# Two depthwise convolutions with group norm: border rows read straight into the taps, small values in PSUM, and a third crossed channel moved from ScalarE and GpSimd to VectorE

## The chip, the cores and the metric

One core of one Trainium2 chip. The metric is device time in microseconds of the core; before the change it was measured three times, with a median of 431.45 us.

## The reference

The input x is 4 x 96 x 128 x 128 in fp32. Twice, the kernel adds to x a convolution of its group norm:

```python
x = x + _L0_conv_ref(_gn(x), w1, w3, w5, alpha)   # alpha0*x + alpha1*dw1(x) + alpha2*dw3(x) + alpha3*dw5(x)
x = x + _L1_conv_ref(_gn(x), w, b)                # one 3x3 filter and one bias for all channels
```

`_gn` takes 32 groups of three channels, each with mean and variance over the three channels and the whole picture. The first convolution is depthwise, and its four terms fold into one 5x5 filter per channel. The second is a 3x3 filter shared by all channels. The kernel calls them X and Y.

## The kernel before

**Tiling.** A unit is two groups, one on partitions 0 to 63 (LO), one on 64 to 127 (HI); each partition holds two picture rows, row p and row p + 64, as two halves of the free dimension, for 4 images and 3 channels of 128 columns. There are 16 units (NU) and 18 periods: in period i the kernel convolves X of unit i and Y of unit i - 2 (LAG). xt holds four pairs of units; x is loaded, updated in place by both convolutions, and stored from it.

**TensorE.** A convolution along the rows is a banded 64 x 64 matrix for each horizontal tap. The normalised input is split into a high and a low fp16 part, gn_hi and gn_lo, and the filter of the high part into two, so a channel takes 15 band products for X and 9 for Y. `tiles` (L382) issues each product as four 64x64 matmuls, two halves of the picture for both groups; for half 1 the output goes to the other group's partitions (LO input to HI output). Those outputs are called crossed. The rows beyond a 64-row strip come through halo, a tile in which each border row stands once for each tap and part, and one more product (`edge`). Group sums over partitions are products with constant matrices (`mean_product`, L443; `var_product`) into the PSUM tile ps_s; it waits for norm_step (L446) before it overwrites ps_s.

**VectorE.** Per period and in this order: `evacuate` of Y's channel 1 of unit i - 3, `deviations` (L652 to L664), Y's channel 2, `affine` (L666 to L688), statistics of x for unit i + 2 (L649), nine evictions for X (three channels, each an uncrossed half on 128 partitions and two crossed quarters on 64), statistics of Y, and Y's channel 0. An eviction (L703) multiplies a PSUM bank by a scale, adds xt and writes xt. In `deviations` the mean is reduced from ps_s, subtracted from the partial means and the difference squared; `affine` turns the variance into g_mul and g_add with a reciprocal and a Newton step. In the last period before the end VectorE also does `whole_part` (L718) and `low_split` (L727) for the last unit, between `affine` and the part (1, 2) of Y's channel 2.

**ScalarE.** `root` (L538), the square root of each unit; `normalize`, 16 activations per period (gn_f in fp32, gn_hi in fp16); `cross_over` (L569), which copies a crossed half of Y from PSUM to the tile cross on the right partitions. With NCROSS = 3 all three channels of Y go this way, and VectorE evicts only their uncrossed halves. The crossing of channel 2 stands right behind `root` of the next period.

**GpSimd.** `low_part` (L870), gn_lo = gn_f - gn_hi, eight per period; `cross_add` (L879), which adds cross to xt.

**SyncE's queue** issues nearly all DMAs in a hand-written order and waits for semaphores in line: `edges_out` (L206, L212, L216) writes the border rows of gn to edge_scratch in DRAM; `edges_spread` (L228) copies them within DRAM to tap_scratch, once per tap and shifted by one column each; `edges_in` (L240, L242) loads tap_scratch to halo, four DMAs; `load_band` (L307) loads the band matrices, `save_pair` (L288) writes filters, `load_pair` (L254) and `store_pair` (L267) move x in and out in alternate periods, batch by batch. In period j the order is: edges_in X of j; edges_out Y of j - 2; bands; filters in even periods; edges_spread Y; load or store of batch 0; edges_in Y; batch 1; edges_out X of j + 1; batch 2; edges_spread X of j + 1; batch 3. A store waits until both the evictions and the cross additions of its unit are done (`unit_ready`). The first four units are loaded one by one, unit 2 by ScalarE's queue (L248); the last unit's border rows go through ScalarE's queue, and so do two of its stores.

## Time and profile before

| | us |
|---|---|
| three runs: lowest, median, highest | 429.09, 431.45, 433.03 |
| the profiled execution | 433.64 |
| its span | 431.8 |
| VectorE busy | 336.6 (78%) |
| TensorE busy | 317.9 (74%) |
| ScalarE busy | 305.3 (71%) |
| GpSimd busy | 261.9 (61%) |

The span runs from the first to the last instruction of the profiled execution. A busy share is an average over start, middle and end, so it doesn't name the limit of any of them; the waits and the timelines do. L-numbers are lines of the kernel before. PE is TensorE, DVE VectorE, ACT ScalarE, POOL GpSimd, SP SyncE; a q behind a name is the queue in which an engine issues DMAs. A bracket at the end of a timeline row is the engine's idle time before it and what ended it.

### The profile page before, as it was taken

The page shows a single profiled execution, that of the slowest core. Times are in us where ns is not written, and L with a number is a line of the kernel's source. Part 1 is how long each engine was busy: PE and PEld are TensorE (multiplying, and loading weights), DVE is VectorE, ACT ScalarE, POOL GpSimd, SP SyncE. Part 2 cuts the span into 40 slices and gives each one's busy share as a digit, 9 for nine tenths or more (in the row PEclk, how much of TensorE's full clock was granted, in tenths as well). Part 3 has the DMA queues.
Part 4 walks back from the last instruction along what each step waited for, and adds up shares of the span by engine and source line. Part 5 has one row for each costly group of instructions (what it writes and reads, how often), then busy time and mean ns, then how long its engine had stood idle before and what let it go on. Part 6 is the DMA issues. An engine that isn't in the chain of part 4 may idle for free.

```text
span 431.8 us, 12518 instructions
## 1 busy us (share of the span) xinstructions
PE 317.9 (74%) x5184; PEld 260.3 (60%) x5184; DVE 336.6 (78%) x667; ACT 305.3 (71%) x374; POOL 261.9 (61%) x207
## 2 busy tenths in 40 slices
PE   2285967819887986988878879688797888983910
PEld 2163645709776865677756767577576788862600
DVE  7868998828979895999699898979898959698110
ACT  1407651499989788779896979697887979835330
POOL 6405632287878676758784867666776868644311
PEclk9997788969999899799989999999899999998865
DMA  7697497104976798678868795779667247404855
GB/s 151 176 241 203 121 230 188 25 31 126 229 188 181 212 218 214 171 216 208 211 174 228 186 241 154 187 209 238 186 178 226 63 142 188 142 18 107 220 144 146
DMA packets 115517, 74.66 MB, mean 173 GB/s; under 512 B 5564, under 2 KB 110916, under 8 KB 115460
## 3 DMA queue, kind: packets, MB, share of 16 engines
q1 hardware_dynamic: 108720, 70.49, 64.2%
q10 hardware_dynamic: 6740, 3.37, 3.4%
q8 instruction: 41, 0.67, 0.7%
q14 instruction: 16, 0.13, 0.1%
HBM read 46.35 MB, written 32.74 MB: 183 GB/s over the span
## 4 chain that ended last, share of the span: by engine, by line
DMA 37%; SPq 29%; DVE 12%; ACT 10%; issue 4%; PE 3%; POOL 2%; ACTq 1%; POOLq 0%
DMA tap_scratch<-edge_scratch 19%; DMA edge_scratch<-gnX 10%; SPq L242 6%; SPq L212 5%; DVE xt L703 5%; SPq L307 5%; ACT gn_f L559 4%; SPq L240 4%; DVE stats L649 4%; ACT gnX L560 3%; DMA xt<-in_x_dram 3%; PE ps L387 3%; SPq L267 2%; SPq L216 2%; SPq L254 2%
## 5 line engine op out<-in xcount | busy, mean ns | idle before, releaser
L387 PE MATMUL ps<-gnX,band 64*64 64x512 f16 x2880 | 187.2, 407 | 28.9 <-DVE xt L703 14.5
L387 PEld LDWEIGHTS ps<-gnX,band 64*64 64x64 f16 x2880 | 157.9, 189 | 53.1 <-issue 39.3
L703 DVE SCALAR_TENSOR_TENSOR xt<-ps,unscale,xt 128x512 f32<-128x512 f32 (+1 forms) x192 | 142.3, 747 | 34.9 <-PE ps L387 32.5
L649 DVE BATCH_NORM_STATS2 stats<-xt 128x6 f32<-128x384 f32 x256 | 121.0, 545 | 17.3 <-DMA xt<-in_x_dram 16.7
L559 ACT ACTIVATE gn_f<-xt,g_add,g_mul 128x768 f32<-128x768 f32 x120 | 122.1, 1017 | 12.6 <-DVE g_add L687 12.0
L870 POOL TENSOR_TENSOR gnX<-gn_f,gnX 128x768 f16<-128x768 f32 x60 | 92.6, 1544 | 60.6 <-ACT gnX L560 60.6
L870 POOL TENSOR_TENSOR gnY<-gn_f,gnY 128x768 f16<-128x768 f32 x60 | 92.6, 1544 | 32.5 <-ACT gnY L560 32.5
L387 PE MATMUL ps<-gnY,band 64*64 64x512 f16 x1728 | 105.3, 386 | 2.1 <-DVE xt L703 2.0
L387 PEld LDWEIGHTS ps<-gnY,band 64*64 64x64 f16 x1728 | 87.0, 187 | 15.7 <-issue 3.9
L879 POOL TENSOR_TENSOR xt<-xt,cross 128x512 f32<-128x512 f32 x48 | 61.3, 1279 | 57.7 <-ACT cross L569 57.3
L569 ACT ACTIVATE cross<-ps,unscale 64x512 f32<-64x512 f32 x96 | 65.5, 682 | 36.7 <-PE ps L387 35.1
L560 ACT ACTIVATE gnX<-xt,g_add,g_mul 128x768 f16<-128x768 f32 x64 | 64.7, 1015 | 1.1 <-DVE g_add L687 1.1
L560 ACT ACTIVATE gnY<-xt,g_add,g_mul 128x768 f16<-128x768 f32 x64 | 64.7, 1015 | 0.0
L538 ACT ACTIVATE std<-var,eps_t 128x8 f32<-128x8 f32 x19 | 5.7, 301 | 61.2 <-DVE var L670 61.0
L387 PE MATMUL ps<-haloX,halo_wX 60*64 60x512 f16 x192 | 18.5, 420 | 19.8 <-DMA haloX<-tap_scratch 19.7
L387 PE MATMUL ps<-haloY,halo_wY 35*64 35x512 f16 x192 | 17.2, 404 | 20.4 <-DMA haloY<-tap_scratch 20.4
L387 PEld LDWEIGHTS ps<-haloY,halo_wY 35*64 35x64 f16 x192 | 6.1, 111 | 26.3 <-DMA haloY<-tap_scratch 23.7
L387 PEld LDWEIGHTS ps<-haloX,halo_wX 60*64 60x64 f16 x192 | 5.4, 110 | 25.5 <-DMA haloX<-tap_scratch 24.8
L449 PE MATMUL ps_s<-stats,ones_mean 64*64 64x32 f32 x76 | 5.8, 224 | 15.7 <-DVE stats L649 15.7
L449 PEld LDWEIGHTS ps_s<-stats,ones_mean 64*64 64x64 f32 x76 | 5.9, 142 | 17.8 <-DVE stats L649 8.8
L456 PE MATMUL ps_s<-stats,ones_var 64*64 64x96 f32 x76 | 7.6, 275 | 11.0 <-DVE stats L663 10.9
L456 PEld LDWEIGHTS ps_s<-stats,ones_var 64*64 64x64 f32 x76 | 5.1, 143 | 16.1 <-DVE stats L663 15.7
(75 smaller groups left out, 107.8 us busy)
## 6 DMA issues: line engine op xcount, KB each, us to landing
out_dram<-xt SPq DMA_DIRECT2D x56, 384.0 KB, 4.7
xt<-in_x_dram SPq DMA_DIRECT2D x48, 384.0 KB, 5.8
band<-diag_scratch SPq DMA_DIRECT2D x48, 160.0 KB, 2.8
tap_scratch<-edge_scratch SPq DMA_DIRECT2D x16, 246.9 KB, 4.1
haloX<-tap_scratch SPq DMA_DIRECT2D x32, 123.4 KB
xt<-in_x_dram SPq DMA_DIRECT2D x20, 192.0 KB, 4.2
xt<-in_x_dram ACTq DMA_DIRECT2D x12, 192.0 KB, 6.6
out_dram<-xt SPq DMA_DIRECT2D x12, 192.0 KB, 3.6
```

The source lines that it names most:

```text
L212: eng.dma_start(edge_dram[s][p, g, :, side, :, :].rearrange("h r e -> r h e"), src).then_inc(edges_landed[s], 16)
L240: eng.dma_start(halo[s][R * g:R * g + 2 * n, p, :, :, :].rearrange("r b c w -> r (b c w)")[:, 0:EDGE], tap_dram[s][p, g, :, :, 0:EDGE].rea ...
L242: eng.dma_start(halo[s][R * g + 2 * n:R * g + 3 * n, p, :, :, :].rearrange("r b c w -> r (b c w)")[:, 0:EDGE], tap_dram[s][p, g, 0, :, 0:E ...
L307: sp.dma_start(band5[:, i % 2, c, :], bass.AP(win.tensor, win.offset + (R // WIN - 1) * NM, [[RUN, 2 * WIN], [-NM, R // WIN], [1, R * NM]] ...
L387: mm = nc.tensor.matmul(ps[to, c, half, :], weights(rows, half), moving(rows, half), start=first, stop=last)
L559: nc.scalar.activation(gn_f[:, f_slot(s, i, b), :, :, :], src, ACT.Identity, **by)
L560: nc.scalar.activation(gn_hi[s][:, i % 2, :, b, :, PAD:PAD + W].rearrange("p e c w -> p c e w"), src, ACT.Identity, **by).then_inc(hi_done ...
L569: cr = nc.scalar.activation(cross[to, c, :, :].rearrange("p b w -> p (b w)"), ps[frm, c, 1, :], ACT.Identity, scale=unscale[frm, NU * CG:N ...
L649: st = nc.vector.bn_stats(stats[:, q_of(at, i) % 2, at, b, e, :], flat[:, SUB * e:SUB * (e + 1)])
L703: ev = nc.vector.scalar_tensor_tensor(out=here, in0=ps[frm, c, half, :].rearrange("h (b w) -> h b w", b=NB), scalar=unscale[rows, at:at + ...
L870: nc.gpsimd.tensor_tensor(gn_lo[s][:, i % 2, :, b, :, PAD:PAD + W].rearrange("p e c w -> p c e w"), gn_f[:, f_slot(s, i, b), :, :, :], gn_ ...
L879: nc.gpsimd.tensor_tensor(here, here, cross[:, c, :, :], ALU.add).then_inc(cross_added, 1)
```

## The change

- `edges_spread` and tap_scratch are gone. `edges_in` stands where edges_spread stood, waits for edge_scratch alone, and reads it with an access pattern of rows, taps (step one element) and columns. In SyncE's order edges_in of Y now stands ahead of batch 0, edges_in of X ahead of batch 3.
- NCROSS is 2. A function `crossed(i, c)` says which channels of Y are crossed by ScalarE and GpSimd: 0 and 1, in the last unit 1 and 2. The other channel's crossed half is evicted by VectorE with two 64-partition evictions, in mid-kernel those of `evacuate(Y, y - 1, 2, (1, 2))`, behind `affine`. The tile cross has two places.
- mean, r0 and dev are now columns 384 and up of the PSUM tile ps_s. `deviations` has one subtraction more (in place in stats), so that the square multiplies dev in PSUM by the difference in SBUF. NORM_OPS is 8. `mean_product` waits for affine_ready of the unit before.
- TensorE runs the 11 warm-up products a second time, behind halo_weights.
- ScalarE waits for unit 1 to have landed before it issues the loads of unit 2.

The diff, with the context lines left out and in `affine` all that is only the renaming of r0 and mean and the count of norm_step:

```diff
@@ -45,7 +45,7 @@
-    NCROSS = 3
+    NCROSS = 2
@@ -60,9 +60,6 @@
-        tap_dram = [nc.dram_tensor(f"tap_scratch{s}", [2, 2, 2, 2 * FAR[s] * len(TAPS[s]), ROW], fp16, kind="Internal").ap()
-                    for s in (X, Y)]
@@ -102,11 +99,8 @@
-        mean = sb("mean", [P, 2 * NB])
-        dev = sb("dev", [P, 8 * NB])
...
-        r0 = sb("r0", [P, 2 * NB])
@@ -114,6 +108,9 @@
+        mean = ps_s[:, 384:384 + 2 * NB]
+        r0 = ps_s[:, 400:400 + 2 * NB]
+        dev = ps_s[:, 416:416 + 8 * NB]
@@ -138,7 +135,6 @@
-        edges_spread_out = [sem(f"edges_spread_out{s}") for s in "XY"]
@@ -155,7 +151,7 @@
-        NORM_OPS = 7
+        NORM_OPS = 8
@@ -187,6 +183,14 @@
+        def crossed(i, c):
...
+            return c < NCROSS if i < LAST else c >= CG - 2
...
+        def crossed_to(i):
...
+            return sum(crossed(n, c) for n in range(i + 1) for c in range(CG))
@@ -217,30 +221,22 @@
-        def edges_spread(eng, s, i):
+        def edges_in(eng, s, i):
...
+            rows = 2 * FAR[s]
+            n = rows * len(taps)
...
-            src = edge_dram[s][p, 0, 0, 0, 0:1, :]
-            dst = tap_dram[s][p, 0, 0, 0:1, :]
-            rows = 8 * FAR[s]
-            eng.dma_start(bass.AP(dst.tensor, dst.offset, [[len(taps) * ROW, rows], [ROW, len(taps)], [1, EDGE]]),
-                          bass.AP(src.tensor, src.offset + taps[0], [[ROW, rows], [1, len(taps)], [1, EDGE]]))\
-               .then_inc(edges_spread_out[s], 16)
...
-        def edges_in(eng, s, i):
...
-            p = i % 2
-            n = 2 * FAR[s] * len(TAPS[s])
-            eng.wait_ge(edges_spread_out[s], 16 * (i + 1))
...
-                eng.dma_start(halo[s][R * g:R * g + 2 * n, p, :, :, :].rearrange("r b c w -> r (b c w)")[:, 0:EDGE],
-                              tap_dram[s][p, g, :, :, 0:EDGE].rearrange("h r e -> (h r) e")).then_inc(halo_in[s][p], 16)
-                eng.dma_start(halo[s][R * g + 2 * n:R * g + 3 * n, p, :, :, :].rearrange("r b c w -> r (b c w)")[:, 0:EDGE],
-                              tap_dram[s][p, g, 0, :, 0:EDGE]).then_inc(halo_in[s][p], 16)
+                src = edge_dram[s][p, g, 0, 0, 0:1, :]
+                for at, parts in ((0, 2), (2, 1)):
+                    eng.dma_start(halo[s][R * g + at * n:R * g + (at + parts) * n, p, :, :, :]
+                                  .rearrange("r b c w -> r (b c w)")[:, 0:EDGE],
+                                  bass.AP(src.tensor, src.offset + taps[0], [[ROW, parts * rows], [1, len(taps)], [1, EDGE]]))\
+                       .then_inc(halo_in[s][p], 16)
@@ -321,9 +317,8 @@
-            edges_spread(sp, X, 0)
+            edges_in(sp, X, 0)
...
-            edges_in(sp, X, 0)
@@ -331,7 +326,7 @@
-                sp.wait_ge(cross_added, NCROSS * (n + 1))
+                sp.wait_ge(cross_added, crossed_to(n))
@@ -350,8 +345,6 @@
-                if 1 <= j < NU:
-                    edges_in(sp, X, j)
@@ -359,16 +352,13 @@
-                    edges_spread(sp, Y, y)
-                in_and_out(j, (0,))
-                if 0 <= y < LAST:
...
-                in_and_out(j, (1,))
+                in_and_out(j, (0, 1))
...
-                    edges_spread(sp, X, j + 1)
+                    edges_in(sp, X, j + 1)
@@ -443,7 +433,7 @@
-                    pe.wait_ge(norm_step, NORM_OPS * (n - 1) + 3)
+                    pe.wait_ge(affine_ready, n)
@@ -483,6 +473,8 @@
+            for _ in range(WARM_UP):
+                nc.tensor.matmul(ps[LO, 2, 0, 0:R], ones_mean[LO, :], ones_mean[LO, :], start=True, stop=True)
@@ -534,7 +526,7 @@
-                act.wait_ge(norm_step, NORM_OPS * n + 3)
+                act.wait_ge(norm_step, NORM_OPS * n + 4)
@@ -564,9 +556,9 @@
-                    act.wait_ge(cross_added, NCROSS * (i - 1) + c + 1)
+                    act.wait_ge(cross_added, NCROSS * (i - 1) + min(c, NCROSS - 1) + 1)
...
-                    cr = nc.scalar.activation(cross[to, c, :, :].rearrange("p b w -> p (b w)"), ps[frm, c, 1, :], ACT.Identity,
+                    cr = nc.scalar.activation(cross[to, c % NCROSS, :, :].rearrange("p b w -> p (b w)"), ps[frm, c, 1, :], ACT.Identity,
@@ -586,6 +578,7 @@
+            act.wait_ge(x_unit_in[0], 128)
@@ -612,12 +605,11 @@
-            edges_spread(act, Y, LAST)
...
-            for c in range(NCROSS):
+            for c in range(CG - 2, CG):
...
-            act.wait_ge(cross_added, NCROSS * NU)
+            act.wait_ge(cross_added, crossed_to(LAST))
@@ -653,14 +645,16 @@
-                nc.vector.tensor_reduce(mean[:, :], ps_s[:, 0:8 * NB].rearrange("h (b e) -> h b e", e=4),
+                nc.vector.tensor_reduce(mean, ps_s[:, 0:8 * NB].rearrange("h (b e) -> h b e", e=4),
...
-                by_sub = dev[:, :].rearrange("h (b e) -> h b e", e=4)
-                mean_of = mean[:, :].unsqueeze(2).to_broadcast([P, 2 * NB, 4])
+                by_sub = dev.rearrange("h (b e) -> h b e", e=4)
+                mean_of = mean.unsqueeze(2).to_broadcast([P, 2 * NB, 4])
...
-                nc.vector.scalar_tensor_tensor(out=halves, in0=by_sub, scalar=float(SUB // 2), in1=by_sub,
+                nc.vector.tensor_tensor(halves, halves, mean_of, ALU.subtract).then_inc(norm_step, 1)
+                dve.wait_ge(norm_step, NORM_OPS * n + 3)
+                nc.vector.scalar_tensor_tensor(out=halves, in0=by_sub, scalar=float(SUB // 2), in1=halves,
@@ -669,29 +663,29 @@
-                nc.vector.reciprocal(r0[:, :], std[:, :]).then_inc(norm_step, 1)
-                dve.wait_ge(norm_step, NORM_OPS * n + 4)
...
+                nc.vector.reciprocal(r0, std[:, :]).then_inc(norm_step, 1)
+                dve.wait_ge(norm_step, NORM_OPS * n + 5)
...
-                moved = s == Y and c < NCROSS
+                moved = s == Y and crossed(i, c)
@@ -874,9 +868,9 @@
-                pool.wait_ge(cross_out, NCROSS * i + c + 1)
+                pool.wait_ge(cross_out, crossed_to(i - 1) + sum(crossed(i, k) for k in range(c + 1)))
...
-                nc.gpsimd.tensor_tensor(here, here, cross[:, c, :, :], ALU.add).then_inc(cross_added, 1)
+                nc.gpsimd.tensor_tensor(here, here, cross[:, c % NCROSS, :, :], ALU.add).then_inc(cross_added, 1)
@@ -930,7 +924,7 @@
-            for c in range(NCROSS):
+            for c in range(CG - 2, CG):
```

## Rows read from the trace of the kernel before

**Rows 1.** The page, part 4: the chain that ended last, share of the span by engine
```profile
DMA 37%; SPq 29%; DVE 12%; ACT 10%; issue 4%; PE 3%; POOL 2%; ACTq 1%; POOLq 0%
```

**Rows 2.** Waits of SyncE's queue, 100 to 389 us: total, times, longest
```profile
SPq L240 <- DMA tap_scratch<-edge_scratch: 31.1, 24, 2.8
SPq L228 <- DMA edge_scratch<-gnX: 18.4, 11, 3.8
```

**Rows 3.** Waits of TensorE, then of VectorE, 100 to 389 us
```profile
PE ps L387 <- DMA haloX<-tap_scratch: 17.3, 11, 3.7
...
DVE stats L649 <- DMA xt<-in_x_dram: 11.0, 5, 3.7
```

**Rows 4.** Timeline of ScalarE: square roots; columns start us, us, engine, line, instruction
```profile
100.04 0.30 ACT L538 ACTIVATE std<-var,eps_t 128x8 f32<-128x8 f32 x1 [0.49 <-DVE var L670]
...
235.52 0.30 ACT L538 ACTIVATE std<-var,eps_t 128x8 f32<-128x8 f32 x1 [2.38 <-DVE var L670]
...
388.72 0.30 ACT L538 ACTIVATE std<-var,eps_t 128x8 f32<-128x8 f32 x1 [2.46 <-DVE var L670]
```

**Rows 5.** Timeline of VectorE, 241 to 258 us
```profile
241.86 6.91 DVE L703 SCALAR_TENSOR_TENSOR xt<-ps,unscale,xt 128x512 f32<-128x512 f32 x9 [1.31 <-PE ps L387]
248.80 3.78 DVE L649 BATCH_NORM_STATS2 stats<-xt 128x6 f32<-128x384 f32 x8
252.50 1.39 DVE L703 SCALAR_TENSOR_TENSOR xt<-ps,unscale,xt 128x512 f32<-128x512 f32 x2
...
254.34 1.19 DVE L661 TENSOR_TENSOR dev<-stats,mean 128x32 f32<-128x32 f32 x1
255.56 1.20 DVE L663 SCALAR_TENSOR_TENSOR stats<-dev 128x32 f32<-128x32 f32 x1
...
257.33 0.21 DVE L670 TENSOR_REDUCE var<-ps_s 128x8 f32<-128x64 f32 x1
257.91 0.20 DVE L672 RECIPROCAL r<-std 128x8 f32<-128x8 f32 x1 [0.37 <-ACT std L538]
```

**Rows 6.** Lines L661 and L703: durations in ns, min/median/max
```profile
L661 DVE TENSOR_TENSOR dev<-stats,mean x19: 194/241/1579, 14.2 to 387.0; 128x32 f32<-128x32 f32 x19
...
L703 DVE SCALAR_TENSOR_TENSOR xt<-ps,unscale,xt x192: 731/748/754, 40.0 to 418.7; 128x512 f32<-128x512 f32 x96, 64x512 f32<-64x512 f32 x96
```

**Rows 7.** Timelines of GpSimd and of SyncE's queue, 244 to 256 us
```profile
244.79 1.54 POOL L870 TENSOR_TENSOR gnX<-gn_f,gnX 128x768 f16<-128x768 f32 x1 [0.29 <-ACT gnX L560]
...
247.71 1.67 SPq L212 DMA_DIRECT2D edge_scratch<-gnX  x4
...
254.34 1.31 SPq L254 DMA_DIRECT2D xt<-in_x_dram  x2
```

**Rows 8.** Timeline of TensorE, 245 to 250 us
```profile
245.29 4.15 PE L387 MATMUL ps<-gnY,band 64*64 64x512 f16 x72
```

**Rows 9.** The chain in order of time: start us, us, what
```profile
249.10 4.60 DMA edge_scratch<-gnX
...
370.33 3.82 DMA haloX<-tap_scratch
```

**Rows 10.** Timelines of VectorE and ScalarE's queue, 0 to 110 us
```profile
27.04 3.78 DVE L649 BATCH_NORM_STATS2 stats<-xt 128x6 f32<-128x384 f32 x8 [3.33 <-DMA xt<-in_x_dram]
...
70.71 3.78 DVE L649 BATCH_NORM_STATS2 stats<-xt 128x6 f32<-128x384 f32 x8 [1.31 <-DMA xt<-in_x_dram]
...
21.71 2.96 ACTq L248 DMA_DIRECT2D xt<-in_x_dram  x3
```

**Rows 11.** The last 40 us: timelines of VectorE, TensorE, GpSimd; one row of the chain
```profile
394.64 3.16 DVE L727 TENSOR_TENSOR gnY<-gn_f,gnY 128x768 f16<-128x768 f32 x2
...
398.31 0.64 PE L387 MATMUL ps<-haloY,halo_wY 35*64 35x512 f16 x4 [7.06 <-DMA haloY<-tap_scratch]
...
418.77 4.06 POOL L879 TENSOR_TENSOR xt<-xt,cross 128x512 f32<-128x512 f32 x3 [11.33 <-ACT cross L569]
...
408.74 2.60 DMA tap_scratch<-edge_scratch
```

More of the change, by code:

```diff
@@ L671, in affine @@
                 dve.wait_ge(std_done, n + 1)
-                nc.vector.reciprocal(r0[:, :], std[:, :]).then_inc(norm_step, 1)
-                dve.wait_ge(norm_step, NORM_OPS * n + 4)
-                nc.vector.scalar_tensor_tensor(out=newton[:, :], in0=var[:, :], scalar=GN_EPS, in1=r0[:, :],
+                nc.vector.reciprocal(r0, std[:, :]).then_inc(norm_step, 1)
+                dve.wait_ge(norm_step, NORM_OPS * n + 5)
+                nc.vector.scalar_tensor_tensor(out=newton[:, :], in0=var[:, :], scalar=GN_EPS, in1=r0,
                                                op0=ALU.add, op1=ALU.mult).then_inc(norm_step, 1)
-                dve.wait_ge(norm_step, NORM_OPS * n + 5)
-                nc.vector.scalar_tensor_tensor(out=newton[:, :], in0=newton[:, :], scalar=-0.5 * G_SCALE, in1=r0[:, :],
+                dve.wait_ge(norm_step, NORM_OPS * n + 6)
+                nc.vector.scalar_tensor_tensor(out=newton[:, :], in0=newton[:, :], scalar=-0.5 * G_SCALE, in1=r0,
                                                op0=ALU.mult, op1=ALU.mult).then_inc(norm_step, 1)
-                dve.wait_ge(norm_step, NORM_OPS * n + 6)
+                dve.wait_ge(norm_step, NORM_OPS * n + 7)
                 for s in (X, Y):
@@ L683, in affine @@
                         dve.wait_ge(hi_done[s], NB * (last + 1))
-                nc.vector.scalar_tensor_tensor(out=g_mul[:, n % 2, :], in0=newton[:, :], scalar=1.5 * G_SCALE, in1=r0[:, :],
+                nc.vector.scalar_tensor_tensor(out=g_mul[:, n % 2, :], in0=newton[:, :], scalar=1.5 * G_SCALE, in1=r0,
                                                op0=ALU.add, op1=ALU.mult).then_inc(norm_step, 1)
-                dve.wait_ge(norm_step, NORM_OPS * n + 7)
-                nc.vector.scalar_tensor_tensor(out=g_add[:, n % 2, :], in0=mean[:, :], scalar=-1.0, in1=g_mul[:, n % 2, :],
+                dve.wait_ge(norm_step, NORM_OPS * n + 8)
+                nc.vector.scalar_tensor_tensor(out=g_add[:, n % 2, :], in0=mean, scalar=-1.0, in1=g_mul[:, n % 2, :],
                                                op0=ALU.mult, op1=ALU.mult).then_inc(affine_ready, 1)
```

## Prediction

> **What bounds the kernel now.** I read the chain that ended last first. It is no compute engine: DMA holds 37% of it and SyncE's queue 29%, and the largest piece, 19%, is the copy of border rows from edge_scratch to tap_scratch [rows 1]. SyncE works in order, so each wait for such a copy also delays the loads and stores written behind it. The waits of that queue from 100 to 389 us say how much: 31.1 us until tap_scratch had landed, 18.4 until edge_scratch had [rows 2]. The compute engines' waits in the same stretch show who pays: TensorE waits 17.3 us for haloX, VectorE 11.0 us for x, five times 2.2 [rows 3].
>
> The pace is the distance between the square roots on ScalarE, one for each unit: 100.04 to 388.72, 288.7 us for 13 periods, 22.2 us each [rows 4]. VectorE's timeline gives what one period needs there: nine evictions of the first convolution 6.91 us (0.768 each), eight statistics 3.7 from start to start (twice in a period), two evictions of Y 1.39, TENSOR_TENSOR L661 1.19, SCALAR_TENSOR_TENSOR L663 1.20 [rows 5]. The last two need not be so long: L661 lies between 0.194 and 1.579 us, median 0.241, while the eviction L703 never leaves 0.731 to 0.754 [rows 6]. L661 and L663 read two SBUF operands, L703 one from PSUM and one from SBUF, and GpSimd works all the while. I take it that the former wait until a GpSimd instruction ends.
>
> **The change, part by part.**
>
> *Border rows straight into the taps.* For each convolution of each unit one DMA and one wait go; edges_in takes the place of edges_spread in SyncE's order and reads edge_scratch with the shift that the spread used. Number and bytes of the halo DMAs stay. SyncE's waits were (31.1 + 18.4) / 13 = 3.8 us of its 22.2; without the spread's part, 2.4, it could run at 19.8. What is late next is the haloX chain. GpSimd ends the last low part of X 10.8 us after the square root (246.33 against 235.52) [rows 4, 7]. L212's four issues take 1.67 us, and b3 of the load starts 6.6 us after they began, straight behind the spread's issue (254.34 against 247.71) [rows 7]. Halos are then asked for at root + 15 to 18 and land by root + 19 to 22. TensorE wants them 6.5 us after the next root, at a period of 20.4 at root + 27: 5 us of cover, and TensorE's waits for halos go.
>
> *Third channel's crossed half on VectorE.* ScalarE loses two activations (1.4 us) and GpSimd an addition (1.3) for each unit; VectorE gains two evictions at 0.768, 1.5 us. ScalarE gains little: behind the root its normalisation waits for g_add, and that takes L672 and four more small steps, over 1 us, anyway; the crossing filled this gap. I count 0.3 us; as it sat idle 2.38 us before the root in a period of 22.1 [rows 4], it needs 19.4. The two new evictions stand behind the affine steps on VectorE; TensorE's third channel waits for them, which end 5.9 us into the period, and it gets there at 9: covered by 3 us.
>
> *Small values in PSUM.* mean, dev and r0 move, so L661, L663 and the last four steps read one SBUF operand at most. One subtraction more is done. Bounds: 0.19 us each (L661 unblocked) to 1.2 (still blocked) [rows 5, 6]. I take 0.23 from start to start, near the 0.21 of reduction L670, which reads PSUM in the same stretch; the far end is a rival below.
>
> *The sum for VectorE*, in us from the eviction of Y's first channel: two evictions and the wait for mean 1.61; mean, two subtractions and the square 0.81; channel 2, plain half 0.66; L670 to L672, with the root, 0.58; reciprocal and four steps 0.92; crossed half 1.5; statistics of x 3.7; nine evictions 6.94; statistics of Y 3.7. Together 20.4 [rows 5]. TensorE sets no more: 72 matmuls take 4.15 us, 57.6 ns each [rows 8], a unit has 312 of them, 18.0 us, and 0.5 for the statistics. Starting 1.0 behind Y's eviction it has X's first channels at 8.9, where VectorE comes at 9.7, and is done at 19.5, where it waits for VectorE until 21.4. In the last two of the 13 periods there are no statistics of x, and TensorE's first channels count: 8.9 + 0.1 + 6.9 + 3.7 = 19.6.
>
> So 11 x 20.4 + 2 x 19.6 = 263.6 where there were 288.7: 25.1 us less. Against it stand the waits for x, 11.0 us [rows 3]. The loads of batches 0 and 1 now start some 4 us ahead of the X edges, which today are issued right behind them; but periods are shorter too. None may be left or all; I keep half, 5.5 us. The middle gives 19.6 us.
>
> On how fast the halo reads are: today's, with 40 and 20 rows in the outer dimension, land in 3.82 us on the chain; the new source has 8, 4 or 2 rows outermost. The nearest row with so few is edges_out itself, 4.60 us behind two loads [rows 9]. I take 4, with 3 and 5 as ends, all inside the cover. The Trainium skill (DMA: Bandwidth & Descriptors, Rules for kernel authors) says that an outermost dimension of fewer than 16 confines a DMA to at most that many engines, and so speaks against these reads. No row shows haloX in that shape; by the rule they would be later, which changes the sum only past the cover.
>
> *The start.* ScalarE now waits until unit 1 has landed before it asks for unit 2. VectorE got unit 1 at 27.04 after 3.33 us of idling; loads of unit 2 were being issued until 24.7 beside it [rows 10]. Unit 1 may come up to 3.3 earlier; I take 2.5. Unit 2's eight DMAs are then issued from 24.5 to about 30.5 and land 4 to 6.6 later, at 34 to 37, where VectorE took them at 34.3. From there it has no gap until it waits 1.31 us for unit 4, at 70.71 [rows 10], which SyncE now asks for some 2 us earlier. From -1.5 to +2: I take 0. The eleven new warm-up matmuls lie in TensorE's idling before the first convolution, at no cost. The stronger wait ahead of the mean product is met a period before.
>
> *The end.* Today TensorE waits 7.06 us for haloY of unit 14, until 398.31 [rows 11], since edges_in stands behind a store that waits for the crossings. Now it stands ahead of it. But VectorE evicts the crossed half of unit 13 only behind whole_part and low_split, which end at 397.8 [rows 11]; two evictions, 399.3, and TensorE's channel 2 waits for these, 0.5 later than today if TensorE starts 0.5 less early. The last spread, 2.60 us, goes. Of the three last additions on GpSimd, 4.06 us [rows 11], two remain: 1.3 less, as VectorE's five last evictions (3.7) end with them. 2.6 + 1.3 - 0.5 - 0.2 for the added subtraction = 3.2 less.
>
> **Sum.** Span 431.8 - 19.6 - 3.2 = 409.0 us. The profiled execution had 433.64 us, 1.84 above its span and 2.2 above the median 431.45 of the runs. 22.8 off the median is 408.6; I say 408.5.
>
> **The rivals.**
> *No wait for x is left.* The forecast less 5.5: 403. For it: SyncE's new slack. 0.22.
> *DMA keeps the load periods.* The other 5.5 us of waits for x stay, and a tenth of those for haloX, 1.7: 408.6 + 7.2 = 416. For it: these waits exist now, and the same loads must land in shorter periods. Against: the spread's traffic goes. 0.20.
> *SyncE's waits were hidden anyway.* Then only the end is shorter: 428. Against: TensorE's waits for haloX [rows 3]. 0.04.
> *Slower: the small steps stay blocked.* If an instruction with one PSUM operand still waits for GpSimd, three of them cost 1.2 to 1.4 instead of 0.23. VectorE then needs 20.4 + 3.2 = 23.6 in eleven periods and 16.7 + 3.2 = 19.9 in two, 299.4 against 288.7: 10.7 more, less the end's 3.2: 439. It decides from 22.5 us a period on, when the three cost 2.8 together. Against: L703, which never waited [rows 6]. 0.05.
> *The forecast.* 0.49, by itself 404 to 413.
>
> The range is 400 to 420. A measurement here tells about 1% from no change. Faster by over 1%: 0.91; within 1%: 0.04; slower: 0.05.
>
> **What would show it.** Right: no L661 or L663 over 0.3 us; roots 20.4 to 21.2 apart; next to no waits of TensorE for haloX; VectorE over 90% busy from 100 to 370; SyncE waiting for GpSimd's low parts rather than for scratch. Wrong: small steps above 1 us; TensorE waiting for halos, or in mid-kernel for channel 2's crossed half; VectorE's waits for x still 2 us; roots 22 us apart while VectorE waits for ps.

## The result and the profile after

The changed kernel takes 439.06 us (median of 4 runs, 436.80 to 440.15) where the kernel before took 430.27 beside it: ratio 1.020, in brackets its 95% interval [1.016, 1.024]. It is slower by 8.8 us; 408.5 was forecast. Medians are over all executions of a kernel, while a ratio and its interval compare only those within 1.5% of the fastest of their kernel. Its profiled execution had 439.24 us, its span 437.4, 5.6 more than the span before. L-numbers are now those of the changed kernel.

The forecast was made in three parts. They are cut at the square roots 5 and 18, counted from 0 (18 is the last); "period" below is the distance between two roots. ScalarE's timeline after gives the cuts, to be read against [rows 4]:

```profile
106.57 0.30 ACT L530 ACTIVATE std<-var,eps_t 128x8 f32<-128x8 f32 x1 [0.85 <-DVE var L664]
...
242.94 0.30 ACT L530 ACTIVATE std<-var,eps_t 128x8 f32<-128x8 f32 x1 [3.38 <-DVE var L664]
263.62 0.30 ACT L530 ACTIVATE std<-var,eps_t 128x8 f32<-128x8 f32 x1 [1.54 <-DVE var L664]
...
394.06 0.30 ACT L530 ACTIVATE std<-var,eps_t 128x8 f32<-128x8 f32 x1 [2.14 <-DVE var L664]
```

| | before | after | difference | forecast |
|---|---|---|---|---|
| start, to root 5 | 100.04 | 106.57 | +6.5 | 0 |
| middle, 13 periods | 288.7 | 287.5 | -1.2 | -19.6 |
| end, from the last root | 43.1 | 43.3 | +0.2 | -3.2 |

So of 22.8 us of gain 21.8 are missing, 18.4 in the middle and 3.4 at the end, and the start costs 6.5 on top. The waits of VectorE, 106.5 to 394 us, then those of TensorE and of SyncE's queue, 100 to 389 us, say what the middle is made of now:

```profile
DVE stats L641 <- DMA xt<-in_x_dram: 16.6, 5, 5.3
DVE var L664 <- PE ps_s L446: 6.6, 5, 1.4
...
DVE xt L697 <- PE ps L377: 4.5, 2, 2.3
```
```profile
PE ps L377 <- DVE xt L697: 39.8, 21, 5.7
PE ps L377 <- ACT cross L561: 9.6, 1, 9.6
```
```profile
SPq L236 <- DMA edge_scratch<-gnX: 18.9, 12, 3.5
SPq L236 <- DMA edge_scratch<-gnY: 8.6, 8, 2.8
```

Nobody waits for haloX any more [rows 3]: TensorE waits for VectorE. The spread's part of SyncE's waits is gone [rows 2]. But VectorE waits 16.6 us for x where it waited 11.0. Of the waits for var 1.4 us lie just ahead of root 5, so between the roots these three lines make 26.3 us. That leaves VectorE 287.5 - 26.3 = 261.2 us of its own, and eleven periods of 20.67 and two of some 16.7 make 260.8: the sum for VectorE was right, the waits beside it were not.

The small steps run as forecast. The two steps that took 1.2 us in [rows 5] now read one operand from PSUM; VectorE's timeline, and the view of line L653 over all 19 units:

```profile
240.03 0.20 DVE L653 TENSOR_TENSOR ps_s<-stats,ps_s 128x32 f32<-128x32 f32 x1
...
240.50 0.20 DVE L657 SCALAR_TENSOR_TENSOR stats<-ps_s,stats 128x32 f32<-128x32 f32 x1
...
242.69 0.23 DVE L664 TENSOR_REDUCE var<-ps_s 128x8 f32<-128x64 f32 x1 [1.32 <-PE ps_s L446]
...
269.45 1.02 DVE L641 BATCH_NORM_STATS2 stats<-xt 128x6 f32<-128x384 f32 x2 [2.94 <-DMA xt<-in_x_dram]
```
```profile
L653 DVE TENSOR_TENSOR ps_s<-stats,ps_s x19: 202/204/209, 14.2 to 392.6; 128x32 f32<-128x32 f32 x19
```

What SyncE does in that pair of periods stands in its queue's timeline. Behind it stands the view of the halo line (durations in ns), and then the line that answers to it in the kernel before:

```profile
246.45 2.65 SPq L236 DMA_DIRECT2D haloY<-edge_scratch  x4
249.15 3.01 SPq L250 DMA_DIRECT2D xt<-in_x_dram  x4
253.43 1.25 SPq L216 DMA_DIRECT2D edge_scratch<-gnX  x4
254.72 1.30 SPq L250 DMA_DIRECT2D xt<-in_x_dram  x2
259.59 2.79 SPq L236 DMA_DIRECT2D haloX<-edge_scratch  x4
262.42 1.35 SPq L250 DMA_DIRECT2D xt<-in_x_dram  x2
```
```profile
L236 SPq DMA_DIRECT2D haloX<-edge_scratch x64: 604/648/1424, 28.8 to 372.6; - x64
```
```profile
L240 SPq DMA_DIRECT2D haloX<-tap_scratch x32: 283/324/1012, 33.8 to 369.9; - x32
```

One halo issue costs SyncE 0.65 us instead of 0.32. With eight of them in a period that is 2.6 us more, against some 1.4 for the two spreads that went (0.71 each, shown further down). And the halo issues stand ahead of batch 3, where one spread stood.

These rows close a loop. Root, 242.94; GpSimd's low parts, then the X edges, 253.43 (10.5 later); they have landed and halos are issued, 259.59 (6.2); batch 3 of x, 262.42 (2.8); VectorE gets it, 269.45 (7.0); the root after next, 287.21 (17.8). Together 44.3 us for two periods, 22.1 each. VectorE's own work fills only the last step and about 1 us behind the first root. The two evictions that it took over stand ahead of the statistics of x, outside the loop. The experiments ask whether this loop or something beside it holds the middle, then what cost the start and the end.

### The profile page after: what moved, and what is told of

It reads as the page before. It is cut to its first block, busy times and chain, and to the rows that moved or that the text cites. A ratio compares the mean times of both kernels' runs of the same rounds, so it can differ in the third digit from the quotient of the medians.

```text
span 437.4 us, 12490 instructions
## 1 busy us (share of the span) xinstructions
PE 321.3 (73%) x5206; PEld 276.3 (63%) x5206; DVE 339.8 (78%) x718; ACT 283.6 (65%) x342; POOL 242.1 (55%) x191
## 4 chain that ended last, share of the span: by engine, by line
DVE 38%; DMA 20%; SPq 13%; ACT 11%; PE 8%; issue 4%; ACTq 2%; POOL 2%; POOLq 0%
DVE xt L697 17%; DVE stats L641 15%; DMA xt<-in_x_dram 10%; PE ps L377 8%; DMA edge_scratch<-gnX 6%; ACT gn_f L551 5%; SPq L236 5%; ACT gnX L552 4%; SPq L216 2%; DMA edge_scratch<-gnY 2%; SPq L250 2%; SPq L263 2%; POOL gnX L864 1%; DMA haloY<-edge_scratch 1%; ACTq L244 1%
## 5 line engine op out<-in xcount | busy, mean ns | idle before, releaser
L377 PEld LDWEIGHTS ps<-gnX,band 64*64 64x64 f16 x2880 | 168.1, 189 | 52.7 <-issue 46.8
L697 DVE SCALAR_TENSOR_TENSOR xt<-ps,unscale,xt 64x512 f32<-64x512 f32 (+1 forms) x224 | 166.1, 747 | 23.0 <-PE ps L377 19.9
L377 PE MATMUL ps<-gnY,band 64*64 64x512 f16 x1728 | 112.1, 401 | 28.1 <-DVE xt L697 28.0
L377 PEld LDWEIGHTS ps<-gnY,band 64*64 64x64 f16 x1728 | 89.1, 189 | 48.8 <-issue 26.5
L561 ACT ACTIVATE cross<-ps,unscale 64x512 f32<-64x512 f32 x64 | 43.7, 683 | 44.6 <-PE ps L377 43.6
L873 POOL TENSOR_TENSOR xt<-xt,cross 128x512 f32<-128x512 f32 x32 | 41.3, 1290 | 42.8 <-ACT cross L561 42.7
L377 PE MATMUL ps<-haloX,halo_wX 60*64 60x512 f16 x192 | 24.1, 391 | 0.0
L648 DVE TENSOR_REDUCE ps_s<-ps_s 128x8 f32<-128x32 f32 x19 | 3.8, 198 | 14.8 <-PE ps_s L439 14.8
L664 DVE TENSOR_REDUCE var<-ps_s 128x8 f32<-128x64 f32 x19 | 4.2, 224 | 8.4 <-PE ps_s L446 8.3
L377 PEld LDWEIGHTS ps<-haloX,halo_wX 60*64 60x64 f16 x192 | 10.3, 109 | 0.3
```

What stands on the lines that cost most here:

```text
L377: mm = nc.tensor.matmul(ps[to, c, half, :], weights(rows, half), moving(rows, half), start=first, stop=last)
L561: cr = nc.scalar.activation(cross[to, c % NCROSS, :, :].rearrange("p b w -> p (b w)"), ps[frm, c, 1, :], ACT.Identity, scale=unscale[frm, ...
L697: ev = nc.vector.scalar_tensor_tensor(out=here, in0=ps[frm, c, half, :].rearrange("h (b w) -> h b w", b=NB), scalar=unscale[rows, at:at + ...
L873: nc.gpsimd.tensor_tensor(here, here, cross[:, c % NCROSS, :, :], ALU.add).then_inc(cross_added, 1)
```

## The experiments

Theory L holds that the middle is paced by the loads of x, late behind SyncE's other work. The rivals blame VectorE's own additional evictions, TensorE's halos, or shared DMA bandwidth. Each text on record says what it expects. Ratios are to the kernel before, run beside each on the same chip; "middle" is as in the table above, between the same two roots. Start, middle, end and waits come from one traced execution of each kernel. How far they scatter: the changed kernel, a1, g1 and g2, alike in the middle, have 287.5 to 289.5 there; kernels with the changed start have root 5 between 101.6 (d1) and 107.2 (c5).

**One part undone at a time.** a1 deletes ScalarE's wait ahead of the loads of unit 2.

```diff
-            act.wait_ge(x_unit_in[0], 128)
```

> The changed kernel without ScalarE's wait for unit 1 ahead of the loads of unit 2. Theory S (the start): this wait alone makes the start 6.5 us longer (root of unit 5 at 106.57 us against 100.04 before; VectorE waits 9.42 us for x of unit 2), so the time falls from 439 to about 433, and VectorE's wait for unit 2 falls under 2 us. Rival R (the start is bound by the bytes of all loads, in whatever order): under 2 us of gain, 437 or more, the wait only moves to unit 1 or unit 3.

436.42 us, 1.011 [1.002, 1.020], between what theory and rival expected. VectorE's wait for unit 2 is gone and root 2 comes at 41.96 instead of 49.98, but VectorE now waits 3.9 us for unit 4. Root 5 comes at 102.80, 3.8 earlier; the middle takes 288.8. So the wait costs something, but 3.8 us of start in one trace, among starts that scatter by 5.6, don't say how much.

a2 crosses all three channels by ScalarE and GpSimd again:

```diff
-    NCROSS = 2
+    NCROSS = 3
```

> The changed kernel with all three channels of Y crossed by ScalarE and GpSimd again (NCROSS = 3), nothing else undone. Theory V (VectorE is the bound of the changed kernel, and the two added evictions of 1.5 us are what took the gain): eleven full periods shorten by 1.2 to 1.5 us, 439 falls by 13 to 16, to 424, and roots lie 20.5 us apart. Rival Q (SyncE's queue and the landing of x are the bound): what VectorE gives up comes back as waits for x; the time falls by 4 us at most, 435 or more.

431.26, 1.001 [0.996, 1.006]. The middle is 286.8, as long as with two crossed channels, though VectorE has 1.5 us a period less to do (it is busy for 227.2 us of the middle instead of 246.9). Its waits for x, 100 to 389 us:

```profile
DVE stats L641 <- DMA xt<-in_x_dram: 35.5, 5, 8.9
```

The 13 x 1.5 us that VectorE got free turned into waiting for x, 18.9 us more of it: it isn't VectorE that paces the middle. Of the 7.8 us by the medians 6.3 are the end, 37.0 instead of 43.3; the start, 2.1 shorter, lies within its scatter.

a3 puts mean, r0 and dev back into SBUF. It was run after the c series, whose periods its text uses.

```diff
-        mean = ps_s[:, 384:384 + 2 * NB]
-        r0 = ps_s[:, 400:400 + 2 * NB]
-        dev = ps_s[:, 416:416 + 8 * NB]
+        mean = sb("mean", [P, 2 * NB])[:, :]
+        r0 = sb("r0", [P, 2 * NB])[:, :]
+        dev = sb("dev", [P, 8 * NB])[:, :]
```

> The changed kernel with mean, r0 and dev in SBUF tiles again, all else kept. The steps that read two SBUF operands are blocked again for up to 1.2 us each, some 1.1 us a period (21.77 against 20.67 between the roots of periods without a wait for x in the pair of kernels with the loads first). Since a pair of periods stays near 45 to 46 us with or without such savings (three crossed channels saved 1.15 us a period and waits for x grew from 16.6 to 35.5 us), both theories expect little: within 4 us of 439. More than 8 us slower would mean that VectorE is the bound after all.

440.57, 1.021 [1.013, 1.029], the ratio of the changed kernel. VectorE's waits for x fall to 9.4 us; the blocked steps come back in their place (L657 takes up to 1.42 us, where it never took over 0.204 with dev in PSUM). The trace is of the slowest execution, 444.18, with a middle of 291.8.

a4 is the kernel before with the direct taps alone (edges_in, its place in SyncE's order, no spread); a5 is the changed kernel with the spread, tap_scratch and the old order back, of which two places:

```diff
-                    edges_in(sp, X, j + 1)
+                    edges_spread(sp, X, j + 1)
...
+                if 1 <= j < NU:
+                    edges_in(sp, X, j)
```

> The kernel before with only the border rows read straight into the taps; crossing, small values and start as before. Theory H: within 3 us of before (430), halo issues at 0.65 us. Rival (the copy's removal pays as forecast where VectorE is not yet loaded further): 418 or less. If it is slower than 433, the halo reads alone carry part of the loss.

> The changed kernel with the copy to tap_scratch and its place in SyncE's order as before, all else as changed. Theory H (halo reads straight from edge_scratch are slow themselves, 0.65 us of issue each against 0.32, and so give back what the copy's removal saved): within 3 us of the changed kernel's 439, and the issues of halo DMAs fall back to 0.3 us. Rival (the removal does help, by SyncE's 2.4 us a period, and something else is worse): slower by 10 us or more, 449, with TensorE waiting for haloX.

a4: 432.31, 1.005 [1.000, 1.009]; middle 288.9, TensorE's waits for haloX gone, those for x 20.8 instead of 11.0, end 37.8. a5: 442.02, 1.021 [1.011, 1.031]; middle 290.1, waits for haloX 24.5, for x 3.6. The direct taps move the wait from haloX to x and leave the middle about where it was, in both kernels.

**The loads moved forward.** c1 issues all four batches ahead of the X edges in load periods; c3 does the same to the kernel before, c4 to a2 without the wait of a1, c5 to a3.

```diff
-                in_and_out(j, (0, 1))
+                in_and_out(j, (0, 1, 2, 3) if j % 2 else (0, 1))
...
-                in_and_out(j, (2,))
+                in_and_out(j, () if j % 2 else (2,))
...
-                in_and_out(j, (3,))
+                in_and_out(j, () if j % 2 else (3,))
```

> The changed kernel with the loads of batches 2 and 3 ahead of edges_out of X in the load periods (odd j), the rest of SyncE's order kept. Theory L (a pair of periods is a loop: root, low part of X, edges_out, landing, halo issues, load of batch 3, its landing, statistics of x, root after next; 46 us whatever VectorE does): the loop is cut, VectorE's waits for x (16.6 us) fall under 3, a pair of periods is set by VectorE at 41.5 to 43 us, and the time falls by 12 to 18 us to 421 to 427. Rival D (DMA bandwidth: the loads cannot land sooner, the same bytes wait elsewhere): 436 or more, with new waits of TensorE for haloX in place of those for x.

> The kernel before with the same reordering of the loads. Theory L: waits for x fall from 11.0 us to under 3, but the spread still stands in the haloX chain and TensorE's waits for haloX (17.3 us) stay or grow; 422 to 428. Rival D: 430 within 1%.

> The changed kernel with the loads first, all three channels crossed by ScalarE and GpSimd, and no wait for unit 1 ahead of unit 2's loads. Theory L: VectorE has 19.5 us a period (seen between 240.8 and 260.3 in the run with three crossed channels), ScalarE 19.2; a pair of periods at 39.5 to 41, time 408 to 416, the fastest of all. Rival D: 428 to 432, as with three crossed channels alone.

> The changed kernel with the loads first and mean, r0 and dev in SBUF tiles again, with the added subtraction. With the loop cut VectorE is the bound, so the small steps that wait for GpSimd show: 1 to 3 us a period, 10 to 30 us slower than the same kernel with them in PSUM. If the loop is not cut (rival D) they hide in the waits for x: under 3 us slower.

All four are slower: 457.63 (1.064 [1.056, 1.072]), 462.07 (1.072 [1.064, 1.080]), 447.29 (1.040 [1.034, 1.047]) and 459.62 (1.067 [1.061, 1.074]). c1's queue, and TensorE's wait, 100 to 389 us:

```profile
262.68 10.69 SPq L250 DMA_DIRECT2D xt<-in_x_dram  x8
273.47 1.38 SPq L216 DMA_DIRECT2D edge_scratch<-gnX  x4
279.32 2.81 SPq L236 DMA_DIRECT2D haloX<-edge_scratch  x4
```
```profile
PE ps L377 <- DMA haloX<-edge_scratch: 47.1, 10, 10.6
```

Eight loads in a row take 10.69 us to issue, 1.34 each, where the pairs and the four shown for the changed kernel took 0.65 to 0.75 each; the edges behind them go out 22.7 us behind the root, 12.2 later than in the changed kernel. Theory L in its simple form, that loads come too late and want to be first, fell; what its rival D expected, new waits for haloX, came. c5 gives the price of the blocked steps where nothing covers it: its uncovered periods take 21.77 us, c1's 20.67. That is 1.1 us a period (from [rows 5] it would be 1.9). In a3, on the changed kernel, eleven such periods add 1.5 us to the median and not 12: most of it is hidden there.

d1 moves only batch 3 ahead of the halo issues, in all periods; d2 does so to the kernel before, d3 to a2 without the wait of a1.

```diff
+                in_and_out(j, (3,))
                 if j + 1 < NU:
                     edges_in(sp, X, j + 1)
-                in_and_out(j, (3,))
```

> The changed kernel with the load or store of batch 3 ahead of edges_in of X, so that it is issued before SyncE waits for the X edges to land. All four loads back to back cost 18 us because the X edges queue behind them; here the edges go out first. Theory L (the loop closes through the load of batch 3 behind edges_in): the load is issued 5 us earlier in load periods, waits for x fall from 16.6 us to under 6, time 425 to 431. Rival D (the DMA engines are what the load and the edges compete for, in either order): haloX is late instead, TensorE waits for it 10 us or more, 436 to 445.

> The kernel before with batch 3 ahead of edges_spread of X. Theory L: VectorE's waits for x (11.0 us) go, but the spread is asked for 1.3 us later in a chain that already makes TensorE wait; 427 to 432. Rival D: slower than 433, with TensorE's waits for haloX over 25 us.

> The changed kernel with batch 3 ahead of edges_in of X, three crossed channels and no wait for unit 1. Theory L: with 19.5 us a period on VectorE and the load earlier, 412 to 420, faster than before. Rival D: 428 to 436.

d1: 439.01 over ten executions, but its ratio, 1.012 [1.003, 1.021], rests on three of them and its trace is of the fastest, 432.00; waits for x 11.1, for haloX 26.3. d2: 464.61, 1.076 [1.065, 1.086]; haloX 42.0. d3: 426.70, 0.986 [0.981, 0.990]; haloX 32.6, in a trace of 429.37 us. Here too one wait is bought with another, as rival D expected.

**Less traffic, or cheaper halos.** In e2 units 8 to 15 load only picture rows 0 to 63, half the bytes in half as many pieces; the rest of xt keeps the values of the units before.

```diff
+                if m >= NX:
+                    eng.dma_start(xt[HALVES[g], m % NX, b, :, :, 0, :].rearrange("p u c w -> p (u c) w"),
+                                  x[b, c:c + 2 * CG, 0:R, :].rearrange("c p w -> p c w")).then_inc(x_in[m % NX], 16)
+                    continue
```

> The changed kernel, where the loads of pairs 4 to 7 bring only rows 0 to 63 of each picture (half the bytes and descriptors, same number of DMAs in the same places; the other half of xt keeps old values). Theory D (the traffic of x in the shared DMA queues sets the landing of X's edges, of the halos and of x, and so the pair of periods): in the last four load periods the waits for x go, pairs fall from 45 to 46 us to VectorE's 41.5 to 43; 426 to 431. Theory S (SyncE's own issue time and its order set the pair, whatever the bytes): pairs stay over 44.5, 436 or more.

In e3 the halo DMAs move the same bytes to the same places from a flat source, 40 or 20 rows in the outer dimension for X, 12 or 6 for Y, out of diag_scratch; the border values are not those of the picture. g1 does the same with a source of the changed kernel's shape (8, 4 or 2 rows outermost, then taps, then columns), but without the shift by one element.

```diff
-                src = edge_dram[s][p, g, 0, 0, 0:1, :]
+                src = diag_dram[0:1, :, :]
...
-                                  bass.AP(src.tensor, src.offset + taps[0], [[ROW, parts * rows], [1, len(taps)], [1, EDGE]]))\
+                                  bass.AP(src.tensor, src.offset, [[ROW, parts * n], [1, EDGE]]))\
```

And g1's lines in place of the last:

```diff
+                                  bass.AP(src.tensor, src.offset,
+                                          [[len(taps) * ROW + 16, parts * rows], [ROW, len(taps)], [1, EDGE]]))\
```

> The changed kernel, where the halo DMAs read rows of 1580 elements, one behind the other, from the saved filters (same bytes, number, places and waits, but a two-dimensional source with 40, 20, 12 or 6 rows outermost; the border values are not used). Theory H (the shape of the direct reads costs): issues fall from 0.65 to 0.3 us, at the end TensorE waits for haloY 3 us less, waits for x shrink, 428 to 433. Rival: issues fall but the pairs of periods stay at 45 to 46, since the edges' landing behind the loads is what counts: 435 to 438.

> As the flat halo reads from the saved filters, but with a source of three dimensions, 8, 4 or 2 rows outermost and the taps a whole row apart, so no shift by one element; bytes, number and places unchanged. If the shape costs: issues at 0.65 us and 436 to 440, as the changed kernel. If the unaligned shift costs: issues at 0.3 us and 422 to 426, as the flat reads. If issues are 0.65 us and the time lies between, both do.

e2: 421.27 (two executions), 0.975 [0.965, 0.985]. The middle takes 269.6 us, most of its periods 20.66, and VectorE waits 1.6 us for x. Yet the four halo issues take the same 2.79 us as in the changed kernel:

```profile
245.36 1.31 SPq L216 DMA_DIRECT2D edge_scratch<-gnX  x4
246.72 1.27 SPq L251 DMA_DIRECT2D xt<-in_x_dram  x2
248.69 2.79 SPq L236 DMA_DIRECT2D haloX<-edge_scratch  x4
```

What shrank is the landing: the X edges are there 2.0 us behind the end of their issue (246.67 to 248.69), where it was 4.9 (254.68 to 259.59). This is the rival of shared DMA bandwidth (theory D on record; its opposite expected 436 or more), and it holds, more strongly than its text expected: with half the traffic of the loads the middle goes down to VectorE's pace, though no halo issue became cheaper.

e3: 423.95 (two executions), 0.981 [0.973, 0.990], middle 276.0. g1: 438.81, 1.022 [1.016, 1.028], middle 287.7, the changed kernel's time. The line of the halo DMAs in e3, then in g1:

```profile
L236 SPq DMA_DIRECT2D haloX<-diag_scratch x64: 283/334/1427, 28.6 to 359.2; - x64
```
```profile
L236 SPq DMA_DIRECT2D haloX<-diag_scratch x64: 605/647/1431, 29.0 to 372.8; - x64
```

Between e3 and g1 only the shape of the source differs, and it makes 0.33 or 0.65 us of an issue and 14.9 us of the kernel by the medians (taken on two chips; by the ratios it is 4%). The shift by one element costs nothing that is seen. It isn't a matter of few rows either: e3's halos of Y have 12 or 6 rows outermost and are cheap too. What g1's source has more is a third dimension.

```profile
L236 SPq DMA_DIRECT2D haloY<-diag_scratch x60: 281/297/974, 79.3 to 376.3; - x60
```

In e3's queue the loop reads:

```profile
239.91 2.91 SPq L250 DMA_DIRECT2D xt<-in_x_dram  x4
246.62 1.16 SPq L216 DMA_DIRECT2D edge_scratch<-gnX  x4
247.82 1.30 SPq L250 DMA_DIRECT2D xt<-in_x_dram  x2
250.01 1.41 SPq L236 DMA_DIRECT2D haloX<-diag_scratch  x4
251.47 1.30 SPq L250 DMA_DIRECT2D xt<-in_x_dram  x2
```

From root (236.13) to edges are 10.5 us as before, but to the halo issues only 3.4 more, to batch 3 1.5, and batches 0 and 1 start 3.8 us behind the root instead of 6.2. Batch 3 is issued from 15.3 us behind the root on instead of 19.5. Of the 4.1 us gained 1.4 are the four halo issues of X; the other 2.8 are the edges' sooner landing, behind batches 0 and 1 that had gone 2.4 us longer ahead (the halos of Y ahead of them are cheaper too). So e3 works in part through what stands in front of the edges in the DMA engines.

**A version that beats both.** f0 is a2 with a1; f1 moves batch 3 ahead of the halo issues too, in load periods alone.

```diff
+                if j % 2:
+                    in_and_out(j, (3,))
                 if j + 1 < NU:
                     edges_in(sp, X, j + 1)
-                in_and_out(j, (3,))
+                if j % 2 == 0:
+                    in_and_out(j, (3,))
```

> The changed kernel with three crossed channels and without the wait for unit 1. If the two costs add (7.8 and 2.6 us as measured alone), 428 to 429; if both are hidden by the same waits for x, 431 as with three crossed channels alone.

> As that one, with batch 3 ahead of edges_in of X in load periods only. With it ahead in all periods TensorE waited 32.6 us for haloX and the time was 426.7; in store periods nothing needs batch 3 early. If the haloX waits of the store periods go and the x waits stay short: 418 to 424. If the load periods alone make the haloX waits: 425 to 428.

f0: 426.45, 0.986 [0.978, 0.995]; middle 285.7. f1: 420.33, 0.973 [0.966, 0.979]: 10.4 us under the kernel before and 18.7 under the changed one, by the medians. Its start is 98.35, its middle 284.1, its end 36.4. The middle is still 14.5 us over what e2 reached.

**The end.** g2 leaves the changed kernel as it is but for the last period, where VectorE evicts the crossed half of unit 13 ahead of `whole_part` and `low_split`.

```diff
+                    evacuate(Y, y - 1, 2, (1, 2))
...
-                evacuate(Y, y - 1, 2, (1, 2))
+                else:
+                    evacuate(Y, y - 1, 2, (1, 2))
```

> The changed kernel, where the last period evicts the crossed half of unit 13's channel 2 ahead of whole_part and low_split. Theory (this order is what the end lost): TensorE's wait of 8.14 us for L697 falls under 1, the last part from the root of unit 18 to the end goes from 43.3 us to 37 to 39, 433 to 435. Rival (the end is bound by the last low parts and halos, 1.5 us later now): under 2 us of gain.

431.42, 1.005 [1.001, 1.008], 7.6 us less than the changed kernel; the end takes 36.7 us. TensorE's timeline at this place, in the changed kernel and then in g2:

```profile
404.95 4.12 PE L377 MATMUL ps<-gnY,band 64*64 64x512 f16 x36 [8.14 <-DVE xt L697]
...
423.15 1.50 PE L377 MATMUL ps<-haloY,halo_wY 35*64 35x512 f16 x12 [6.92 <-DMA haloY<-edge_scratch]
```
```profile
397.12 2.27 PE L377 MATMUL ps<-gnY,band 64*64 64x512 f16 x36 [0.29 <-DVE xt L697]
```

## Why the prediction was wrong

The direction was wrong: 0.91 stood on faster by over 1%. The slower rival, small steps still blocked, was not what happened. Two steps failed: that SyncE's cost for the halo issues stays, and that half of the waits for x go. Point by point:

*VectorE's need.* Right: 20.4 forecast, 20.67 measured, wherever nothing else is waited for. e2, with fewer bytes to load, shows it: 263.6 us were forecast for the middle without waits for x, and its 269.6 less 1.6 for x and 2.7 for var are 265.3. That the whole forecast, with its 5.5 us for x, was 269.1 is a coincidence.

*TensorE's waits for halos go.* Right, and worth nothing by itself: a4 shows that they turn into waits for x.

*"Number and bytes of the halo DMAs stay."* This is the first step that failed. They do stay, and I took from it that their cost on SyncE stays. It doubles, 0.32 to 0.65 us an issue, by shape alone (e3 against g1), and it doubles in the queue that I had named as the bottleneck: my 22.2 - 2.4 = 19.8 us for SyncE left 1.2 us a period out. I had weighed the shape only for the time of landing, "all inside the cover"; TensorE's waits for haloX did not show it. The kernel before had a row that hints at the price. The spread's source had the same three dimensions, rows, taps and columns (though more rows in one DMA), and its issue took twice a halo's:

```profile
L228 SPq DMA_DIRECT2D tap_scratch<-edge_scratch x31: 543/707/1312, 31.0 to 383.2; - x31
```

With flat halos, e3, 11.5 of the middle's missing 18.4 us come back. That does not make 11.5 the price of the issues alone: e2 gets 17.9 back at the same issue price, so both shorten one loop and their gains don't add up. The Trainium skill (DMA: Bandwidth & Descriptors, Rules for kernel authors) has the rule on an outermost dimension under 16, which I put aside as mattering only past the cover. It speaks of engines, not of issue time, and the issue time does not follow it: the 12 and 6 rows of e3's haloY are under 16 and take 0.30 us. Whether the rule lengthens the landings here no run shows.

*"I keep half, 5.5 us" of the waits for x.* The second step that failed: 16.6 measured. My argument was that batches 0 and 1 start ahead of the X edges. They do, by 4.3 us (249.15 against 253.43), but behind the root they start at +6.2, where batch 0 started at +7.2 (242.75) before. Batch 3 went from root + 18.8 to root + 19.5. The rival "DMA keeps the load periods" had the mechanism and too small a price, 7.2 us: it kept the waits at today's 11 us, and never let them grow as VectorE got faster. I had reckoned SyncE by the waits it has, but a queue that works in order, waits for a landing, and delays the very load that leads to the next root is a loop with its own length. a2 shows it: some 19 us less for VectorE, 19 more of waiting for x, the same 287 us. And two of the loop's steps are landings behind the loads' own traffic, which e2 shortens; "the spread's traffic goes" was too little against that.

*The wait for var.* Not foreseen, 5.2 us in four periods of the middle. TensorE now idles longer before X of a period, and the products behind it run slower. Its timeline there after and before, and for the stretch behind the idling a table of windows, after and then before (the last three columns are the granted clock, the DMA share and GB/s):

```profile
239.18 0.49 PE L377 MATMUL ps<-gnX,band 64*64 64x512 f16 x4 [1.96 <-DVE xt L697]
```
```profile
231.19 0.49 PE L387 MATMUL ps<-gnX,band 64*64 64x512 f16 x4 [0.50 <-DVE xt L703]
```

```profile
239.20:242.40 3.20, 3.20 (x41) 2.73 (x45) 1.84 (x6) 0.37 (x1) 1.88 (x2) 0.59 0.56 170
```
```profile
231.20:234.00 2.80, 1.96 (x32) 1.55 (x32) 2.51 (x4) 1.91 (x3) 2.11 (x2) 1.00 0.93 237
```

The granted clock was 0.59, mostly at the 1.2 GHz level, where it was 1.00. `var_product` comes 1.3 us late by it. It doesn't follow each time: 22.0 us later TensorE idled the same 1.96 us, kept 1.00, and no wait came. The same 24 products, first there and then here:

```profile
239.55 2.88 PE L377 MATMUL ps<-gnX,band 64*64 64x512 f16 x24
...
261.55 1.73 PE L377 MATMUL ps<-gnX,band 64*64 64x512 f16 x24
```

Of seven idlings of 1.96 or 1.97 us between 124 and 285 us three were followed by a clock of 0.50 to 0.61 and a wait for var, four by 1.00 and none; what decides it is not shown. So of the 18.4 us, 11.1 are x, 5.2 are var and 2.1 the rest; in a2 there is no wait for var in the middle and it is as long, so removing it alone would probably only lengthen the wait for x.

*The start, "I take 0".* +6.5. Unit 1 did come earlier, 24.07 against 27.04, as said. Unit 2 did not land "at 34 to 37" but at 42.20. VectorE's timeline:

```profile
42.20 3.78 DVE L641 BATCH_NORM_STATS2 stats<-xt 128x6 f32<-128x384 f32 x8 [9.42 <-DMA xt<-in_x_dram]
```

Its loads were asked for in time (24.07 to 29.8), but now beside the band matrices, the first halos and unit 3, whose eight issues took 10.13 us on SyncE; the landing takes 12.4 us instead of the 4 to 6.6 that I had from quieter rows. Without the wait, a1, root 5 comes 3.8 us earlier; what the other 2.7 are is not shown, and both are within the scatter of the starts.

*The end, "0.5 later".* The working named the place, two evictions behind `low_split`, and took both that step's 3.16 us and the idle time from the kernel before. In fact `low_split` took 4.23 us and TensorE stood 8.14 us; g2 gives 6.6 of the end back by moving the two evictions alone. These products hold up ScalarE's crossings, which stand ahead of the last `edges_out` in its queue: that begins 15.6 us behind the last root (409.67), in g2 10.8 (404.92). From there to TensorE's last halo product it is 12.9 us before, 13.5 after and 12.1 in g2: without the spread's 2.60 us the four halo reads take 8.9 and 6.0 us from first issue to landing, where they took 5.2 before, and little or nothing of those 2.60 is left. So the gain foreseen for the end was there to be had (36.7 us in g2, 37.8 in a4, 43.1 before), for the most part by other steps than I had reckoned.

What stays open: how the 14 us between f1 and e2 could be had without loading less, whether flat halos (e3's shape needs a staged copy, or other weights) pay once that copy is counted, and how the loop's excess splits into dearer issues, landings of the halos and landings behind the loads. None was tried.

## What to carry to other kernels

An access pattern's shape has a price on the queue that issues it, apart from its bytes: look up the duration of an issue of that shape before a staging copy is traded for it, above all where that queue is the bottleneck. Where an in-order queue waits for a landing and then issues what leads to the next such wait, add up that loop, with landings as long as they are behind the traffic of the same stage, as one more rival to each engine's sum; work taken from an engine that is not the longest only becomes waiting. And an operation that is moved behind another for the steady state has to be followed through the last period separately, where what stands ahead of it is different.

## What the runs showed of the hardware

- The issue of a halo DMA on SyncE takes 0.33 us (X, to 40 or 20 partitions) or 0.30 us (Y, to 12 or 6) from a source of rows and columns (e3), and 0.65 or 0.63 us from one of rows, taps and columns (g1), for the same bytes.
- An issue takes longer when much is in flight. Eight loads of one unit took SyncE 5.32 us for unit 1 and 10.13 for unit 3, while unit 2's, issued by ScalarE, were still landing. In c1 the first four of a pair's eight took 0.66 to 0.79 us each, the last four 1.49 to 2.86.
- The X edges landed 4.9 us behind the end of their issue in the changed kernel, under batches 0 to 2, 2.2 us in e3, where batches 0 and 1 had gone 2.4 us longer ahead, and 2.0 in e2, where they had half the bytes: what stands in front in the DMA engines counts, whatever the size of the transfer.
- With dev in PSUM the subtraction L653 never went over 0.209 us beside a busy GpSimd, where it took up to 1.58 on SBUF alone [rows 6]. With dev back in SBUF in the same kernel, a3, it took up to 1.26. The Trainium skill (SBUF — State Buffer, SBUF: two separate sides) has a VectorE instruction with two SBUF inputs contend for one port pair with a GpSimd instruction that reads SBUF, the loser blocked for the whole instruction; these rows agree.
